# A tiled graph attention with a mixture of experts: block maxima and softmax sums turned on VectorE and by DMA in place of TensorE

## The reference, cut to what matters

```python
lQ = masked_x @ Wlq; lK = x @ Wlk; lV = x @ Wlv + blv
local_scores = where(adj, lQ @ lK.T * scale, -1e9)
max_score = maximum(max(local_scores, axis=1), maximum(global_scores, es))
le = exp(local_scores - max_score)
ge = exp(global_scores - max_score); ee = exp(es - max_score)
denom = sum(le, axis=-1) + ge + ee
res = le / denom @ lV + ge / denom * gV + ee / denom * eV
x_recon = maximum(res, masked_x)
# then layer norm, attention weights, expert MLP with gelu, last layer with gelu
```

## Time and profile before

| what | value |
| --- | --- |
| median of the timed runs | 1141.05 us (1138.73, 1141.05, 1141.51) |
| span of the profiled execution, first to last instruction | 1135.6 us |
| the profiled execution's own time | not given by the page; the median lies 5.4 us above the span |
| busy share of the span | PE 94%, PE weight loads 78%, DVE 76%, POOL 63%, ACT 50% |
| period of one block in the middle of the attention | 89.20 us |

### The profile page before, as it was taken

How to read it: one execution, slowest core, us unless ns; L and a number is a source line. 1 busy time by engine, 2 the same in 40 slices (tenths; PEclk the granted TensorE clock), 3 DMA queues, 4 the chain that set the end, 5 groups by cost and what they waited for, 6 DMA issues and landing times.

```text
span 1135.6 us, 15919 instructions
## 1 busy us (share of the span) xinstructions
PE 1062.2 (94%) x5060; PEld 882.4 (78%) x5060; DVE 865.9 (76%) x1523; ACT 563.5 (50%) x994; POOL 720.0 (63%) x713
## 2 busy tenths in 40 slices
PE   5887999999999999999999999988778899999997
PEld 4665788888888888888888888866666788888886
DVE  4768988798788888888878878978355776678653
ACT  5544254444444444444445443565546456655673
POOL 4755687686787677778777777775454355554551
PEclk8989999999999999999999999999889999999999
DMA  8693533343444443443444435477624636654521
GB/s 263 215 326 147 185 131 130 131 167 140 140 158 141 156 160 130 154 163 121 144 166 139 148 110 171 136 263 268 233 88 153 230 108 238 223 174 148 180 75 56
DMA packets 102087, 187.71 MB, mean 165 GB/s; under 512 B 10226, under 2 KB 41843, under 8 KB 101747
## 3 DMA queue, kind: packets, MB, share of 16 engines
q1 hardware_dynamic: 102002, 186.69, 47.9%
HBM read 147.29 MB, written 30.98 MB: 157 GB/s over the span
## 4 chain that ended last, share of the span: by engine, by line
PE 78%; DVE 8%; issue 4%; DMA 3%; ACT 3%; POOL 3%; SPq 1%; DVEq 0%; ACTq 0%; POOLq 0%
PE u_ps L1379 19%; PE s_ps L50 11%; PE s_ps L52 11%; PE s_ps L51 11%; PE u_ps L1386 10%; PE u_ps L50 2%; PE u_ps L52 2%; PE u_ps L51 2%; PE mb_ps L50 1%; PE mb_ps L51 1%; DMA v_scratch<-vst 1%; PE mb_ps L52 1%; DVE h_lo L846 1%; PE mt_ps L50 1%; PE s_ps L1443 1%
## 5 line engine op out<-in xcount | busy, mean ns | idle before, releaser
L598 POOL TENSOR_TENSOR p_lo<-p_all,p_hi 128x512 fp32r<-128x512 f32 x247 | 325.2, 1317 | 191.9 <-PE u_ps L1386 125.3
L1127 ACT ACTIVATE p_hi<-scores 128x512 fp32r<-128x512 f32 x256 | 161.7, 632 | 357.2 <-DVE scores L755 338.0
L1379 PE MATMUL u_ps<-p_hi,v_in 128*128 128x512 f32 x1024 | 277.3, 393 | 6.8 <-DMA v_in<-v_scratch 6.0
L769 DVE TENSOR_TENSOR scores<-s_ps,bias 128x512 f32<-128x512 f32 x256 | 175.6, 686 | 96.2 <-PE s_ps L52 85.9
L1379 PEld LDWEIGHTS u_ps<-p_hi,v_in 128*128 128x128 f32 x1024 | 191.2, 189 | 46.8 <-DMA v_in<-v_scratch 6.8
L50 PE MATMUL s_ps<-q_hi,lnT_hi 128*128 128x512 f32 x512 | 203.3, 397 | 10.3 <-DVE scores L769 8.3
L52 PE MATMUL s_ps<-q_hi,lnT_lo 128*128 128x512 f32 x512 | 201.5, 393 | 0.0
L51 PE MATMUL s_ps<-q_lo,lnT_hi 128*128 128x512 f32 x512 | 201.2, 393 | 0.0
L755 DVE TENSOR_TENSOR scores<-scores,mb_ps 128x512 f32<-128x512 f32 x256 | 171.6, 677 | 0.8 <-PE mb_ps L1405 0.8
L591 POOL TENSOR_SCALAR bias<-adj 128x512 f32<-128x512 uint8 x256 | 163.9, 641 | 13.1 <-DVE scores L769 13.1
L783 DVE TENSOR_TENSOR kept_ps<-kept_ps,scores 128x512 f32<-128x512 f32 x232 | 162.3, 699 | 8.0
(11 more groups left out here) (190 smaller groups left out, 1642.6 us busy)
## 6 DMA issues: line engine op xcount, KB each, us to landing
v_in<-v_scratch SPq DMA_DIRECT2D x128, 512.0 KB, 3.7
adj<-in_adj SPq DMA_DIRECT2D x64, 256.0 KB, 3.8
raw<-in_wffn SPq DMA_DIRECT2D x32, 512.0 KB, 4.8
v_scratch<-vst SPq DMA_DIRECT2D x8, 1024.0 KB, 6.0
mx<-in_mx SPq DMA_DIRECT2D x18, 256.0 KB, 6.8
xg<-in_x SPq DMA_DIRECT2D x8, 512.0 KB, 6.1
mg_raw<-in_mxT SPq DMA_DIRECT2D x16, 256.0 KB, 3.8
uhi_scratch<-uT_high SPq DMA_DIRECT2D x8, 512.0 KB, 2.7
```

The lines of the kernel that those rows point to most:

```text
L598: nc.gpsimd.tensor_tensor(out=p_lo[:, y % 2], in0=p_all[:, y % 2], in1=p_hi[:, y % 3].bitcast(fp32), op=ALU.subtract).then_inc(plo_ready, 1)
L769: nc.vector.tensor_tensor(scores[:, t % SLOTS], s_ps[t % 3][:, :], bias[:, t % 2], ALU.add).then_inc(masked, 1)
L1127: nc.scalar.activation(p_hi[:, y % 3], scores[:, y % SLOTS], ACT.Exp, scale=SCALE).then_inc(phi_ready, 1)
L1379: nc.tensor.matmul(u_ps[d][:, :], v_in[:, i % VRING, x % 2, at:at + P], p_hi[:, x % 3], start=k == 0 and part == 0, stop=False)
```

## The change

The block maxima no longer pass through TensorE. A 32 by 32 transpose of VectorE turns each 32 x 32 square of a 128 x 512 tile in place. `fold_tops` (DVE, step k = 1, where `pick_top` stood) turns `top_keys` into `mt_ps`, reduces it to 16 numbers per partition, copies the three upper quarters of the partitions under the lowest one, lays the extra scores' maxima beside them in four copies, and reduces the five parts to `block_top` (32 x 16). `spread_tops` (DVE, at the end of step k = 2) copies `block_top` to the three other quarters, copies it wide into `top_spread`, writes `top` in four copies, and turns `top_spread` into `mb_ps`. The sums are turned by two DMAs on SyncE: the row goes to DRAM (one step after its block has ended) and comes back as a column of 128 x 4 (three steps after). `low_result` waits for the first DMA and `shares` for the second; `low_result`, `shares`, `scaled_rows` and `extra_rows` are two steps later, the stores of `uT` three and of the coefficients two; the last block's `shares` moves from place j = 0 to j = 1 of the first expert.

```diff
+    sum_dram = scratch("sum_scratch", (BLOCKS, CH))
...
+                def store_sums(n):
+                    sp.wait_ge(u0_copied, n + 1)
+                    sp.dma_start(sum_dram[n:n + 1], uT[0:1, 0, :]).then_inc(row_stored, 16)
+                def load_sums(n):
+                    sp.wait_ge(row_stored, 16 * n + 16)
+                    wait(sp, den_ready, n - 1)
+                    sp.dma_start(sums[:, n % 2], sum_dram[n].rearrange("(t p) -> p t", p=P), allow_slow_non_contiguous=True).then_inc(sums_loaded, 16)
...
+                    ended = ends_block(t - 1)
+                        store_sums(ended)
                     ended = ends_block(t - 3)
+                        load_sums(ended)
+                    ended = ends_block(t - 6)
                         sp.wait_ge(ulow_ready, 2 * ended + 2)
...
                 def low_result(n, k):
-                    pool.wait_ge(sum_done, n + 1)
+                    pool.wait_ge(row_stored, 16 * n + 16)
...
-                        ended = ends_block(t - 1 - d)
+                        ended = ends_block(t - 3 - d)
                             low_result(ended, d)
...
-                def pick_top(n):
+                def fold_tops(n):
+                    dve.wait_ge(kept, LASTS * n + LASTS)
+                    nc.vector.transpose(mt_ps[:, :], top_keys[:, :]).then_inc(turned, 1)
+                    dve.wait_ge(extra_topped, n + 1)
+                    for a in range(TG):
+                        nc.vector.tensor_copy(quarters[0:32, TG, a::TG], extra_top[32 * a:32 * a + 32, n % 2, :]).then_inc(extra_laid, 1)
                     dve.wait_ge(turned, n + 1)
-                    nc.vector.tensor_reduce(local_top, mt_ps[:, :].rearrange("p (t q) -> p t q", t=TG), AX.X, ALU.max).then_inc(local_ready, 1)
-                    nc.vector.tensor_tensor(top[:, n % 2], local_top, extra_top[:, n % 2], ALU.max).then_inc(top_ready, 1)
-                    nc.vector.tensor_copy(top_spread[:, :, :], top[:, n % 2, :].unsqueeze(2).to_broadcast([P, TG, P])).then_inc(spread_ready, 1)
+                    nc.vector.tensor_reduce(quarters[:, 0], mt_ps[:, :].rearrange("p (b j) -> p b j", j=32), AX.X, ALU.max).then_inc(quarter_ready, 1)
+                    dve.wait_ge(quarter_ready, n + 1)
+                    for a in range(1, TG):
+                        nc.vector.tensor_copy(quarters[0:32, a], quarters[32 * a:32 * a + 32, 0]).then_inc(quarters_laid, 1)
+                    dve.wait_ge(quarters_laid, 3 * n + 3)
+                    dve.wait_ge(extra_laid, 4 * n + 4)
+                    nc.vector.tensor_reduce(block_top[0:32, :], quarters[0:32, :, :].rearrange("p a b -> p b a"), AX.X, ALU.max).then_inc(quarter_top, 1)
+                def spread_tops(n):
+                    dve.wait_ge(quarter_top, n + 1)
+                    for a in range(1, TG):
+                        nc.vector.tensor_copy(block_top[32 * a:32 * a + 32, :], block_top[0:32, :]).then_inc(top_copied, 1)
+                    dve.wait_ge(top_copied, 3 * n + 3)
+                    nc.vector.tensor_copy(top_spread[:, :].rearrange("p (b j) -> p b j", j=32),
+                                          block_top[:, :].unsqueeze(2).to_broadcast([P, KT // 2, 32])).then_inc(spread_ready, 1)
+                    for a in range(TG):
+                        nc.vector.tensor_copy(top[32 * a:32 * a + 32, n % 2, :], block_top[32 * a:32 * a + 32, a::TG]).then_inc(top_ready, 1)
+                    dve.wait_ge(spread_ready, n + 1)
+                    wait(dve, centred, KT * n)
+                    nc.vector.transpose(mb_ps[:, :], top_spread[:, :]).then_inc(spread_done, 1)
...
-                    dve.wait_ge(sum_done, n + 1)
-                    nc.vector.tensor_tensor(den, sum_bank(n)[:, 0:TG], extra_sum, ALU.add).then_inc(den_ready, 1)
+                    dve.wait_ge(sums_loaded, 16 * n + 16)
+                    nc.vector.tensor_tensor(den, sums[:, n % 2], extra_sum, ALU.add).then_inc(den_ready, 1)
...
-                        if e == 0 and j == 0:
+                        if e == 0 and j == 1:
                             shares(BLOCKS - 1)
...
-                        pick_top(n - 1)
+                        fold_tops(n - 1)
                     for y in centred_in(t):
                         centre(y)
                     if t < TILES:
                         mask(t)
                         keep(t)
+                    if n > 0 and k == 2 and n <= BLOCKS:
+                        spread_tops(n - 1)
...
-                def turn_tops(n):
-                def spread_tops(n):
-                def add_up(n):
...
```

More of the change, by code:

```diff
@@ L260, in gnn_moe_kernel @@
         late_low_ready = sem("late_low_ready")
-        turned, local_ready, top_ready, spread_ready, spread_done = (
-            sem(n) for n in ("turned", "local_ready", "top_ready", "spread_ready", "spread_done"))
+        turned, quarter_ready, extra_laid, quarters_laid, quarter_top, top_copied, top_ready, spread_ready, spread_done = (
+            sem(n) for n in ("turned", "quarter_ready", "extra_laid", "quarters_laid", "quarter_top", "top_copied",
+                             "top_ready", "spread_ready", "spread_done"))
         extra_dotted, extra_topped, gap_ready, extra_exped = (
@@ L266, in gnn_moe_kernel @@
             sem(n) for n in ("u0_copied", "u1_copied", "uhigh_ready", "ulow_ready", "u_stored"))
-        sum_done, gsum_ready, den_ready, rden_ready, coef_ready, coef_stored = (
-            sem(n) for n in ("sum_done", "gsum_ready", "den_ready", "rden_ready", "coef_ready", "coef_stored"))
+        row_stored, sums_loaded, gsum_ready, den_ready, rden_ready, coef_ready, coef_stored = (
+            sem(n) for n in ("row_stored", "sums_loaded", "gsum_ready", "den_ready", "rden_ready", "coef_ready", "coef_stored"))
         STEPS = TILES + LAG
@@ L525, in _ @@
                 sp.dma_start(b2_c[:, :], b2).then_inc(b_loaded, 16)
-                for t in range(KT, STEPS + 8):
+                for t in range(KT, STEPS + 9):
                     n, k = divmod(t, KT)
@@ L543, in _ @@
                             load_masked_rows(sp, m // 4, m % 4)
+                    ended = ends_block(t - 1)
+                    if ended is not None:
+                        store_sums(ended)
                     ended = ends_block(t - 3)
+                    if ended is not None:
+                        load_sums(ended)
+                    ended = ends_block(t - 6)
                     if ended is not None:
@@ L548, in _ @@
                         sp.dma_start(ulo_dram[ended], uT_low[:, :, :].bitcast(fp32)).then_inc(u_stored, 16)
-                    ended = ends_block(t - 6)
+                    ended = ends_block(t - 8)
                     if ended is not None:
@@ L552, in _ @@
                         sp.dma_start(coef_dram[ended], coefs[:, 0:3]).then_inc(coef_stored, 16)
-                    ended = ends_block(t - 20)
+                    ended = ends_block(t - 22)
                     if ended is not None and ended < BLOCKS - 1:
@@ L807, in top_extra @@
                     dve.wait_ge(extra_dotted, 8 * n + 8)
+                    wait(dve, extra_laid, 4 * n - 4)
                     nc.vector.tensor_tensor(extra_top[:, n % 2], extras[:, n % 2, 0], extras[:, n % 2, 1], ALU.max).then_inc(extra_topped, 1)
                 def gap_extra(n):
-                    dve.wait_ge(top_ready, n + 1)
+                    dve.wait_ge(top_ready, 4 * n + 4)
                     wait(dve, extra_exped, n)
@@ L1102, in _ @@
                             top_extra(n)
-                    ended = ends_block(t - 4)
+                    ended = ends_block(t - 6)
                     if ended is not None:
                         shares(ended)
-                    ended = ends_block(t - 17)
+                    ended = ends_block(t - 19)
                     if ended is not None:
@@ L1339, in _ @@
                         high_result(ended)
-                    ended = ends_block(t - 14)
+                    ended = ends_block(t - 16)
                     if ended is not None:
@@ L1642, in _ @@
                         score(t)
[L1643 to L1646, removed]
                     if t >= LAG:
                         weigh(t - LAG)
-                    ended = ends_block(t)
-                    if ended is not None:
-                        add_up(ended)
                     beside(t - LAG - LAST)
```

19 lines of the change are left out of this document (5 added, 14 removed).

## The result

The changed kernel takes **1172.27 us** (median of four, 1171.85 to 1173.55) beside 1139.89 for the kernel before (four runs): ratio 1.0284, 95% interval 1.0264 to 1.0305, so 32.4 us slower. The forecast was 1165 in a range of 1140 to 1177: the sign and the main waits are right, the increase is 8.6 short (+32.4 where +23.8 stood).

What follows compares the result with a forecast made beforehand. TensorE, busy for all 89.20 us of a block, was taken to bound the kernel. Inner changes 22.2, first change 4.1, last change 1.0 and first expert -3.5 gave +23.8 on 1141.05: 1165 us, range 1140 to 1177.

Steps and rivals of the forecast that it cites:

- the deadline: Step 5 of a new block: TensorE's next `weigh` waits for VectorE's `take_second`; 4.3 us of wait in all.
- VectorE's work: Change of block: fold and spread take 5.4 us where 1.26 stood; 4.2 are left, so TensorE waits 1.2.
- Short copies: Rival at the change of block: small copies take 0.07 each and wait for GpSimd; 1150 us, chance 0.21.
- dearer transposes: Rival in fold and spread: two-pass transposes of 1.40 us each, 11 us more in all; 1176 us, chance 0.12.
- Copies behind GpSimd: Fold and spread: SBUF-to-SBUF copies wait for GpSimd's `p_lo` and bias, 1.5 and 1.6, together 3.1 us.
- copies that don't wait for GpSimd: Rival at the change of block: copies of 0.19 us, not held, and the clock stays; 1140 us, chance 0.13.
- TensorE's relief: Each block: the three pieces taken from TensorE give back at most 2.14 us.
- The clock: Behind TensorE's wait at each change of block: a stretch at lower clock loses 1.5 us, bounds 0 and 1.7.
- DMAs and GpSimd: Inside the blocks: small DMAs hidden, `low_result` beside `low_queries` absorbed by about 3 us of room for `p_lo`; cost 0.
- The sum: Six inner changes of block: 2.2 us longer plus 1.5 of clock each, +22.2 us.
- The first change: First change of block: nothing weighed yet, VectorE alone is the path to the first `p_lo`; +4.1 us, no saving.
- The last change: Last change of block: VectorE 4.5 us later, against `add_up` 1.0 and `extra_rows` 2.5; +1.0. First expert separately -3.5.

Runs made afterwards that it cites:

- run 4: The changed kernel with both halves of `u_ps` copied by ScalarE in `take_first` instead of VectorE's `take_second`: 1174.85 us.
- run 3: The changed kernel with its fourteen small VectorE copies a block written as maxima over an axis of one element: 1138.95 us.
- Run 9: The changed kernel with GpSimd's `low_queries` for the next block three steps later, at steps 13 and 14 instead of 10 and 11: 1167.52 us.
- run 5: The changed kernel with both copies of `u_ps` on ScalarE, one step earlier, ahead of the new block's second exponential: 1156.07 us.

## Why the prediction was right, and where its size came from

- **What bounds the kernel, and the deadline.** Right: TensorE full before, and `take_second` where it waits, 3.94 for 4.3 (4.1 from where the next product would have started). What the text did not see is that the deadline is not that copy alone: in the changed kernel ScalarE's copy, behind exponentials that wait for VectorE, ends only 0.4 us ahead of it, and when it has both copies the wait is 4.0 (run 4).
- **VectorE's work.** 5.26 for 5.4, where nothing holds it: transposes 0.72 and 0.73 (0.70 said), L827's four copies of 0.15 to 0.17 at a pitch of 0.19 (0.19 said). Short copies and dearer transposes, two of the rivals, are out.
- **Copies behind GpSimd.** 2.9 a change for 3.1; the third and fourth copies of the fold, as said, and the first and second of the spread instead of the second and third. Shown by run 3. The rival of copies that don't wait for GpSimd is what run 3 built: 1138.95, where that rival had 1140.
- **TensorE's relief.** 2.14 was said; 89.21 less 384 products at 0.2267 is 2.2. Only the first of the six periods gives less, 1.5: no `add_up` stood in it.
- **The clock: mis-sized.** 1.5 was said; the half-clock stretches behind the six waits cost 1.4 to 1.7 and 2.5 to 2.9 in turn, at 0.2 a product, mean 2.1. The two rows behind that estimate were a stretch of 3 us and a window that mixes both levels.
- **DMAs and GpSimd: the step that failed.** They were costed at 0, with 3 us of room for `p_lo`. The transfers were indeed hidden (the load back from `sum_scratch` lands in 2.1 to 4.5 us, and TensorE has no new wait on a value load in the blocks). But `low_result`'s move, next to `low_queries` as the text says, and that of `shares`, which it doesn't weigh at all, make TensorE wait for `p_lo`: by the starts of products some 0.75 us in each of five blocks, 3.7 in all (the sixth block has no next queries). Run 9, in which that wait is gone, is 4.8 us faster, its half-clock stretches being others too. With it the windows close: 87.05 of products, 4.1 of wait, 0.75, and 1.7 or 2.6 of clock are 93.6 and 94.5. GpSimd's queue was counted, VectorE's instructions that it holds were not.
- **The sum.** The six inner periods are 4.2 to 5.5 longer than before, 29.0 in all for 22.2. Of the 6.8, by the starts of products, 3.8 is the clock, 3.7 `p_lo` and 0.5 a smaller relief, less 1.2 for waits a little shorter than said. The first change: 4.11 more from its `mask` to the first `centre`, 4.1 said. The last change: +3.9 to the last `weigh` (4.4 in its period, -0.5 in the drain) for +3.5 without `extra_rows`; behind it -4.4, for -6.0 with `extra_rows` and the first expert, where VectorE no longer waits at `shares`. With the 2.4 below and 0.6 gained between the first `centre` and the first `weigh`, these add up to 34.4 of the 34.5.
- **Not explained:** 2.4 of the 34.5 us are there before the first `fold_tops`; the first `weigh` lies between 133 and 142 us in the thirteen traces, and of it I tried nothing.

## What to carry to other kernels

Work that is taken off a full engine pays only if the engine that gets it keeps the deadline in the very step, so cut the profile at the change of block and add up what stands in order there, held copies included. Before a small copy is put beside a busy GpSimd, choose its form: in these runs a reduction over an axis of one element, or an input from PSUM, was not held where a copy or two SBUF inputs were. And when steps are moved to make room for a change, price each move on its own: the two-step moves here cost 4 to 5 us, and moving another pair by three steps gave them back.

## What was not expected of the hardware

What a wait of TensorE cost besides itself differed more than the waits: after 1.44 us the next four products took 1.16 instead of 1.07; after 2.1 (run 5) eight products started 0.2 us late each behind five of the six waits, and the sixth cost only 0.1; after 3.94 it was about 1.6 and 2.6 us from block to block in turn. What differs there is when the clock fell: at the change at 421.35 it stood at 0.50 from 419.9 on, 1.4 us before the first product, at the change at 327.75 it was still 1.00 up to 327.6. And `add_up`, eight one-column products, took 1.86 instead of 1.05 at the half clock.
